# Where the two batches of an expert are cut: 256 and 384 rows in place of 320 and 320, and four experts split at the front in place of three

## The reference, cut to what matters

```
capacity = int(s * K / E * CAP_FACTOR)               # 1024*2/8*1.25 = 320 rows of each expert and batch
dispatch = einsum('bsm,bsec->ebcm', hidden_states, dispatch_mask)
h1 = einsum('ebcm,emh->ebch', dispatch, w1)          # 256 -> 896
h3 = einsum('ebcm,emh->ebch', dispatch, w3)
expert_out = einsum('ebch,ehm->ebcm', silu(h1) * h3, w2)   # 896 -> 256
final = einsum('ebcm,bsec->bsm', expert_out, combine_mask)
```

## Time and profile before

| | |
|---|---|
| time, median of 3 runs | 1856.06 us (1853.22 to 1858.87) |
| profiled execution, first to last instruction | 1860.8 us |
| mean granted TensorE clock | 0.929 |
| TensorE busy | 1600.7 us (86%) |
| VectorE busy | 1042.4 us (56%) |
| ScalarE busy | 876.0 us (47%) |
| GpSimd busy | 572.3 us (31%) |
| ffn passes (L1930) | 896, 254.1 us busy |
| y passes (L1940) | 630, 140.6 us busy |

### The profile page before, as it was taken

The page is one execution under the profiler, slowest core; times in us unless marked ns, Lnnn a source line. Parts: engine busy times, 40 slices in busy tenths (PEclk is TensorE's granted clock), DMA queues, the critical chain, the costliest instruction groups (busy, mean ns, idle before and its releaser), DMA issues. The chain is left out here.

```text
span 1860.8 us, 34549 instructions
## 1 busy us (share of the span) xinstructions
PE 1600.7 (86%) x12872; PEld 1085.8 (58%) x12872; DVE 1042.4 (56%) x2132; ACT 876.0 (47%) x1458; POOL 572.3 (31%) x823
## 2 busy tenths in 40 slices
PE   4668989978669999999985569999999999997888
PEld 2423333336546777777652357777777777776544
DVE  4557777716242111111244687888888878882656
ACT  2105666662232111111123467888888778872331
POOL 2301111112412200000233455555555555543111
PEclk9759999997778999999986889999999999998899
DMA  2461112012102133222112768868778687655101
GB/s 85 115 176 22 23 25 42 1 42 85 53 8 91 57 130 105 88 81 88 45 51 86 220 184 202 208 197 199 203 203 210 192 199 200 191 149 174 46 12 34
DMA packets 208006, 210.33 MB, mean 113 GB/s; under 512 B 19523, under 2 KB 186065, under 8 KB 207713
## 3 DMA queue, kind: packets, MB, share of 16 engines
q1 hardware_dynamic: 202977, 194.49, 38.3%
q0 software_dynamic: 4864, 13.64, 2.2%
HBM read 126.06 MB, written 81.81 MB: 112 GB/s over the span
## 5 line engine op out<-in xcount | busy, mean ns | idle before, releaser
L1197 DVE CUSTOM_DVE_ANT_0 prob<-ps,dev 128x1024 f32<-128x1024 f32 x256 | 311.5, 1217 | 2.1 <-DMA skew_p<-prob 2.0
L1094 ACT ACTIVATE prob<-prob,nmax 128x1024 f32<-128x1024 f32 x256 | 293.3, 1146 | 18.1 <-DVE nmax L1197 17.8
L1026 PE MATMUL ps<-cst,prob 128*128 128x128 f32 x2048 | 278.9, 277 | 1.7 <-issue 1.0
L1930 PE MATMUL ps<-xeT,w 128*128 128x320 f32 x896 | 254.1, 445 | 0.9 <-ACT xeT L1965 0.9
L1026 PEld LDWEIGHTS ps<-cst,prob 128*128 128x128 f32 x2048 | 227.3, 141 | 45.0 <-issue 22.6
L744 ACT ACTIVATE pT<-ps 128x512 f32<-128x512 f32 (+3 forms) x384 | 166.1, 495 | 152.4 <-PE ps L704 150.0
L1211 DVE COPY probT<-ps 128x512 f32<-128x512 f32 x256 | 176.3, 689 | 106.4 <-PE ps L1026 106.4
L781 DVE TENSOR_REDUCE nmax<-ps 128x1 f32<-128x128 f32 (+7 forms) x256 | 185.3, 754 | 81.8 <-PE ps L685 80.6
L1930 PEld LDWEIGHTS ps<-xeT,w 128*128 128x128 f32 x896 | 174.2, 196 | 75.8 <-issue 8.8
L1977 ACT ACTIVATE xT_c<-ps 128x320 f32<-128x320 f32 (+1 forms) x91 | 45.4, 499 | 330.2 <-PE ps L1930 330.2
L1101 ACT ACTIVATE probT<-ps 128x512 f32<-128x512 f32 x256 | 151.2, 591 | 105.2 <-PE ps L1026 105.2
(11 more groups left out here) (310 smaller groups left out, 2222.4 us busy)
## 6 DMA issues: line engine op xcount, KB each, us to landing
dev<-skew_u SPq DMA_DIRECT2D x128, 256.0 KB, 3.8
skew_p<-prob SPq DMA_DIRECT2D x128, 256.0 KB, 3.2
w<-in_L_ffn_w SPq DMA_DIRECT2D x27, 896.0 KB, 6.0
skew_u<-cst SPq DMA_DIRECT2D x64, 256.0 KB, 4.0
wr<-skew_p SPq DMA_DIRECT2D x128, 128.0 KB, 2.9
qs<-qd SPq DMA_DIRECT2D x96, 128.0 KB, 3.8
ks<-kd SPq DMA_DIRECT2D x48, 256.0 KB, 5.8
qd<-parts SPq DMA_DIRECT2D x16, 384.0 KB, 2.5
```

Of the source, the lines that this page charges most:

```text
L1026: last = nc.tensor.transpose(ps[:, ring_bank(job), kb * P:(kb + 1) * P], prob_tile(t, (4 * h + kb) * P, (4 * h + kb + 1) * P), k.c("ident"))
L1094: nc.scalar.activation(prob_tile(t, 0, S), prob_tile(t, 0, S), ACT.Exp, bias=nmax[:, t % 4:t % 4 + 1], scale=-1.0).then_inc(s_exp, 1)
L1197: nc.vector.tensor_tensor_reduce(out=prob_tile(t, 0, S), in0=scores, in1=dev_tile(t), scale=-1.0, scalar=3.0e38, op0=ALU.add, op1=ALU.min, ...
L1930: last = nc.tensor.matmul(ps[:, a + z * wide + h, 0:CAP], w[:, j, c, f * P:(f + 1) * P], xeT[:, c, h * CAP:(h + 1) * CAP], start=(c == 0), ...
```

## The change

An item now names its parts as (batch, first row, rows). Experts 0 to 3 first run with 256 rows of batch 0; then experts 3, 2, 1, 0 run with the other 64 rows of batch 0 and the 320 of batch 1, 384 rows together. Experts 4 and 5 stay wide. Experts 6 and 7 run with the 320 rows of batch 0 and 64 of batch 1, and then with the other 256 rows of batch 1. There are 14 items in place of 13 (12 narrow, 2 wide), 98 ffn units in place of 91, and 40 tiles of y, all of 128 rows, in place of 45. The stores and the loads of rows are 32 pieces as before. The weights are loaded ten times in place of nine (experts 0 and 1 twice). The adds of batch 0 now both stand in the last item: the first four row tiles behind unit 1, the other four behind unit 6.

```diff
-    AHEAD = 3
-    items = ([(e, (0,)) for e in range(AHEAD)] + [(e, (1,)) for e in reversed(range(AHEAD))] +
-             [(e, (0, 1)) for e in range(AHEAD, E - 2)] + [(E - 2, (0,)), (E - 1, (0,)), (E - 2, (1,)), (E - 1, (1,))])
+    AHEAD = 4
+    EVEN = CAP // P * P
+
+    items = ([(e, ((0, 0, EVEN),)) for e in range(AHEAD)] +
+             [(e, ((0, EVEN, CAP - EVEN), (1, 0, CAP))) for e in reversed(range(AHEAD))] +
+             [(e, ((0, 0, CAP), (1, 0, CAP))) for e in range(AHEAD, E - 2)] +
+             [(e, ((0, 0, CAP), (1, 0, CAP - EVEN))) for e in (E - 2, E - 1)] +
+             [(e, ((1, CAP - EVEN, EVEN),)) for e in (E - 2, E - 1)])
+    height = [sum(rows for _, _, rows in parts) for _, parts in items]
+    banks_of = [-(-n // 512) for n in height]
...
-    tiles = [[(o, min(P, CAP * len(h) - o)) for o in range(0, CAP * len(h), P)] for _, h in items]
+    tiles = [[(o, min(P, n - o)) for o in range(0, n, P)] for n in height]
...
-                        j, wide = use[n] % 2, len(items[n][1])
+                        j, wide, cols = use[n] % 2, banks_of[n], height[n] // banks_of[n]
...
-                                    last = nc.tensor.matmul(ps[:, a + z * wide + h, 0:CAP], w[:, j, c, f * P:(f + 1) * P],
-                                                            xeT[:, c, h * CAP:(h + 1) * CAP], start=(c == 0), stop=(c == DC - 1))
+                                    last = nc.tensor.matmul(ps[:, a + z * wide + h, 0:cols], w[:, j, c, f * P:(f + 1) * P],
+                                                            xeT[:, c, h * cols:(h + 1) * cols], start=(c == 0), stop=(c == DC - 1))
...
-                        if n >= len(items) - 2 and f == FC0 - 1:
-                            g = n - len(items) + 2
+                        if n == len(items) - 1 and f in (1, FC0 - 1):
+                            g = int(f > 1)
                             for t in range(4 * g, 4 * g + 4):
                                 add(t)
                             summed(g)
```

More of the change, by code:

```diff
@@ L1806, in banks @@
             first = (2 if n < split else 4) * (own.index(jobs[i]) % 2)
-            return list(range(first, first + 2 * len(items[n][1])))
+            return list(range(first, first + 2 * banks_of[n]))
         bank = [banks(i) for i in range(len(jobs))]
@@ L1830, in pieces @@
         def pieces(n):
[L1832 to L1835, removed]
+            cut, at = [], 0
+            for b, r, left in items[n][1]:
+                while left:
                     p = at % P
-                    rows = min(P - p, CAP - r)
-                    count = (CAP - r) // P if p == 0 and rows == P else 1
+                    rows = min(P - p, left)
+                    count = left // P if p == 0 and rows == P else 1
                     cut.append((b, r, p, rows, at // P, count))
-                    at, r = at + rows * count, r + rows * count
+                    at, r, left = at + rows * count, r + rows * count, left - rows * count
             return cut
@@ L1971, in _ @@
                         _, n, f = step
-                        wide = len(items[n][1])
+                        wide, cols = banks_of[n], height[n] // banks_of[n]
                         z = place(step) - 1
@@ L1976, in _ @@
                             act.wait_ge(s_hT, z - 1)
-                        nc.scalar.activation(sg[:, z % 2, 0:CAP * wide].rearrange("p (h m) -> p h m", h=wide),
-                                             ps[:, a:a + wide, 0:CAP], ACT.Silu).then_inc(s_silu, 1)
+                        nc.scalar.activation(sg[:, z % 2, 0:height[n]].rearrange("p (h m) -> p h m", h=wide),
+                                             ps[:, a:a + wide, 0:cols], ACT.Silu).then_inc(s_silu, 1)
                     elif kind not in ("y", "warm"):
@@ L2062, in _ @@
                         _, n, f = step
-                        wide = len(items[n][1])
+                        wide, cols = banks_of[n], height[n] // banks_of[n]
                         z = place(step) - 1
                         dve.wait_ge(s_silu, z + 1)
-                        nc.vector.tensor_tensor(hT[:, f, 0:CAP * wide].rearrange("p (h m) -> p h m", h=wide),
-                                                ps[:, a + wide:a + 2 * wide, 0:CAP],
-                                                sg[:, z % 2, 0:CAP * wide].rearrange("p (h m) -> p h m", h=wide), ALU.mult).then_inc(s_hT, 1)
-                        if n >= len(items) - 2 and f == FC0 - 1:
-                            g = n - len(items) + 2
+                        nc.vector.tensor_tensor(hT[:, f, 0:height[n]].rearrange("p (h m) -> p h m", h=wide),
+                                                ps[:, a + wide:a + 2 * wide, 0:cols],
+                                                sg[:, z % 2, 0:height[n]].rearrange("p (h m) -> p h m", h=wide), ALU.mult).then_inc(s_hT, 1)
+                        if n == len(items) - 1 and f in (1, FC0 - 1):
+                            g = int(f > 1)
                             for t in range(4 * g, 4 * g + 4):
@@ L2078, in _ @@
                             dve.wait_ge(s_yst, 16 * parts_of(n - 1))
-                        wide = ps[:, a:a + 2 * len(items[n][1]), :].rearrange("p a n -> p (a n)")
+                        wide = ps[:, a:a + 2 * banks_of[n], :].rearrange("p a n -> p (a n)")
                         whole = sum(w == P for _, w in tiles[n])
```

## The result

The changed kernel takes 1842.02 us in the median (four runs, 1841.38 to 1843.45), the kernel before beside it 1857.46 (1853.22 to 1860.25): ratio 0.9923, 95% interval 0.9905 to 0.9941, or 15.4 us less. A second set of runs (six after, eleven before) gave 1844.47 against 1856.7: ratio 0.9928 (0.9907 to 0.9950), 12.2 us less. Forecast were 1845.2 and 10.9 us less. The profiled execution has a span of 1839.6 us, against 1860.8.

A forecast was written before the change was run, and what follows sets the result against it. In the experts TensorE's issued passes were taken as the bound; -17.5 + 1.0 - 1.5 + 4.7 + 2.9 - 0.5 = -10.9 us, from 1856.06 to 1845.2, with 8 in 10 between 1839 and 1853.5.

The forecast's parts named there:

- five pairs: Experts 0, 1, 2, 6, 7 cut as 256 + 384 rows: 3.5 us less a pair, -17.5 (-14.5 to -19).
- expert 3 as a pair: Expert 3 as two items where it was one wide item: 48.20 against 47.24 us, +1.0 (0.6 to 1.6).
- item 0 beyond its pair's share: Item 0's units at half clock shorten more than the pair's sum books: -1.5 us (bounds +2.9 to -3).
- wait behind the adds: Last item: units 2 to 6 queue behind batch 0's adds on VectorE, TensorE stands: +4.7 us (3.5 to 5.5).
- clock behind that wait: Last item: after TensorE's stall, renewed work runs at half clock: +2.9 us (0 to 3.4).
- the end: Last copy and store: VectorE 0.5 us late, no 64-row part, store in one piece: -0.5 us (-1 to +0.5).
- the two bounds: Saving per pair: 3.8 us if the extra is the 64-row tile's, 2.9 to 3.1 if a group's fixed start.
- rival 1: Last item: the clock holds through the stall, or the stall is covered: -13.8 to -18.5 us, 1838 to 1842; 12%.
- rival 2: Item 0 gets colder, its y runs at half clock: +6.1, so -4.8 us, 1851; 15%.
- rival 3: ffn: a pass of 256 columns costs no less than one of 320; kernel +6.7 us, 1862.8; 5%.
- rival 4: Late load (expert 1's second) or late gathers (last item), with loss of clock: +2 to +6 us; 8%.
- SyncE's wait for batch 1: SyncE waits for batch 1's scatter before item 4 in place of item 3: costs nothing.

The follow-up runs named there:

- experiment 4: The kernel before, with the third tile of y of its ten narrow items taken as 128 columns in place of 64: stage 453.29 us, 2.9 less.
- Experiments 2 and 3: Changed kernel with batch 0's adds behind unit 6 of the last two items: stage 437.14 us; changed kernel with ten useless matmuls filling the wait: stage 441.90.
- experiment 8: Both kernels profiled twice more, no edits: stage 455.8 and 452.6 us before, 443.9 and 444.3 changed.

## Why the prediction was right, and where it was short

The mechanism is the one forecast, term by term (us):

| term | forecast | measured |
|---|---|---|
| five pairs | -17.5 | -18.5 (51.72 to 48.02 each) |
| expert 3 as a pair | +1.0 | +0.8 (47.24 to 48.02) |
| item 0 beyond its pair's share | -1.5 | -1.6 (75.52 to 67.40 is -8.1, of which 25.86 - 19.39 = 6.5 is the share) |
| item 1's low clock | none | +0.75 (27.46 is 1.60 above an item before, 21.74 is 2.35 above one after, which begins with a granted clock of 0.50) |
| wait behind the adds | +4.7 | +4.4 |
| clock behind that wait | +2.9 | +2.6 |
| the end | -0.5 | -0.7 (start of y to the gather 14.10 to 10.25; y's passes -3.2) |
| sum | -10.9 | -12.2; the stage as one -12.0 |

Measured is the first profile of each kernel; in the means of four the stage is 11.0 us shorter.

- *Pairs.* The pass for half a tile was the right price, and the choice between the two bounds was too cautious: experiment 4 shows that nearly the whole extra, 0.34 us, belongs to the 64-row form. (The price of a column in the ffn is 0.84 to 0.85 ns by the earlier trace rows; the 0.82 comes from no row.)
- *Item 0.* The four slow units became 2.5 us shorter (16.39 to 13.91) and not 3.3; y began 4.66 us earlier, with 4.4 forecast. That the whole term fits so well is in part luck of the executions: to item 1 the kernel before takes 75.5, 75.1, 75.1 and 71.5 us in its four profiles, and against the last the term would be +2.4.
- *The adds.* The queue behind VectorE's adds, the bank of unit 2 and the loss of clock came as forecast. Experiments 2 and 3 take them apart: 7.0 us of stage, of which the clock is about a third. The Trainium skill (TensorE: Matmul & The Clock Gate, Loop structure matters more than you think) shows TensorE going cold in a loop with a long wait for a DMA ahead of every matmul. Here a single wait of 4.4 us for VectorE was enough: the granted clock fell to 0.50 in it.
- *Rivals.* The clock did not hold through the wait (rival 1); y(0) ran at the full clock (rival 2); 256 columns cost 12.09 us an ffn, no floor (rival 3); neither load nor gather came late (rival 4).
- *SyncE's wait for batch 1.* That it costs nothing before item 4 was right. That four at the front are needed was never argued; with three it costs nothing either.
- *Short by 1.3 to 4.5 us.* The step that was left unsaid, and that the runs don't bear out, is that everything outside the stage takes the same time. In four profiles of each kernel the stretch behind is 6.2 us shorter after the change; 2.0 of that are lost again ahead of the stage and between the two. That it lies there is measured; the part that goes with the code's own loading is argued in experiment 8, and the rest has no known cause. No term of the prediction accounts for it.

The changed kernel so leaves 7 us in its last item and about 1 at its front. With the adds behind the last two items it takes 1836.0 us with four experts ahead and 1833.97 with three, each beside 1856.7 of the kernel before: less than both kernels, and between them no difference that the ratios show.

## What to carry to other kernels

Where an engine is bound by passes, count tiles, not rows: a tile of 64 rows cost the passes of a full one and 0.34 us more, and cutting 640 rows at a multiple of 128 gave 3.7 us a time without a column less of arithmetic. Where work is moved into a shorter loop, look at what queues behind it on its own engine: 6.7 us of adds cost nothing beside a y of 9.4 us and 7 us inside an ffn, a third of it by the clock that the wait brought down. Before paying for cover, measure how much is needed: the landing time of a load is that of its own stretch, not the median over the kernel.

## What the runs showed of the hardware

The length of item 0 hangs on how long the clock stays at its lower level in that execution. With the same instructions it took 57 us to its y in three profiles of the kernel before and 53 in a fourth (two other kernels with that front gave 57.0 and 53.1). In the fourth, three of its units are shorter. The timeline of TensorE there, with the two long waits:

```profile
537.91 1.07 PE L1500 MATMUL ps<-cst,x_sc_c 128*77 128x128 f32 x4 [2.53 <-DVE x_sc_c L1666]
...
540.49 2.79 PE L1930 MATMUL ps<-xeT,w 128*128 128x320 f32 x8
...
551.94 1.11 PE L1483 MATMUL ps<-cst,xn_c 128*128 128x128 f32 x4 [3.92 <-POOL xn_c L1572]
552.85 3.42 PE L1930 MATMUL ps<-xeT,w 128*128 128x320 f32 x8
...
559.20 2.40 PE L1930 MATMUL ps<-xeT,w 128*128 128x320 f32 x8
```

The units were 4.38, 4.22 and 4.09 us in the earlier trace rows. The waits between them are the same, 2.53, 3.92 and 0.69 us; the level of the clock behind them differs. The windows of the first and the last of these units, in the first profile and then in the fourth (columns as above, the granted clock third from the end):

```profile
544.00:546.00 2.00, 2.00 (x6) 1.22 (x5) 0.52 (x2) 0.00 (x0) 0.00 (x0) 0.50 0.00 0
...
566.00:568.00 2.00, 2.00 (x5) 1.31 (x4) 0.00 (x0) 0.00 (x0) 0.00 (x0) 0.51 0.00 0
```

```profile
542.00:544.00 2.00, 2.00 (x10) 1.54 (x9) 0.22 (x1) 0.68 (x2) 0.00 (x0) 1.00 0.00 0
...
560.00:562.00 2.00, 2.00 (x12) 1.48 (x12) 0.00 (x0) 0.36 (x1) 0.00 (x0) 1.00 0.00 0
```

Seven profiles with 256 rows in item 0 all lie at 52.1 to 52.5.
